# Patch embedding in 98 tiles of 128 patches across image borders, and v's product in the bank of o

## The reference, cut to what matters

```python
patches = patchify(images)                       # 64 x 196 patches x 768
hidden = einsum('npd,hd->nph', patches, W_lin) + b_lin
h = concatenate([cls, hidden], axis=1)           # 64 x 197 tokens x 192
h = h + attention(layernorm(h))                  # 12 heads of 16, q and k normalised by head
h = h + experts(layernorm(h))                    # gate, 8 routed experts and a shared one
```

## Time and profile before

| | |
|---|---|
| median of two runs | 1674.95 us (1672.44 and 1677.46) |
| the profiled execution | 1680.21 us, its span 1678.0 us |
| mean granted clock of TensorE in it | 0.984 |
| PE, DVE, ACT, POOL busy, share of the span | 96%, 76%, 59%, 40% |
| first stage / second stage | about 950 us / about 728 us |

### The profile page before, as it was taken

One profiled execution on the slowest core, in us unless ns is written; L12 is line 12 of the kernel. 1 busy time (PEld: TensorE's weight loads), 2 busy tenths in 40 slices (PEclk: granted clock), 3 DMA queues, 4 the chain that ended last, 5 costly groups with the idle time before them and its releaser, 6 DMA issues. The chain is left out here.

```text
span 1678.0 us, 44146 instructions
## 1 busy us (share of the span) xinstructions
PE 1611.4 (96%) x16714; PEld 1104.3 (66%) x16714; DVE 1275.9 (76%) x3610; ACT 987.5 (59%) x2038; POOL 676.0 (40%) x758
## 2 busy tenths in 40 slices
PE   4999999999999999999998799999999999999998
PEld 4777777777777777777776455555555555555555
DVE  5787777777777777777775488888888878888877
ACT  2777777777777777777766344454545454444543
POOL 2333333333333333333332155554545545555543
PEclk8999999999999999999998599999999999999999
DMA  7233333333333333333310111112121211111110
GB/s 242 69 78 78 78 78 78 78 78 78 78 78 78 78 78 78 78 78 78 106 42 19 30 42 40 56 39 57 36 61 33 58 39 45 52 42 55 34 35 16
DMA packets 97695, 108.11 MB, mean 64 GB/s; under 512 B 61323, under 2 KB 74286, under 8 KB 97358
## 3 DMA queue, kind: packets, MB, share of 16 engines
q1 hardware_dynamic: 88270, 85.83, 17.3%
q0 software_dynamic: 9216, 19.47, 7.6%
HBM read 92.44 MB, written 19.37 MB: 67 GB/s over the span
## 5 line engine op out<-in xcount | busy, mean ns | idle before, releaser
L1407 POOL TENSOR_TENSOR in_lo<-inner,in_hi 128x512 f16<-128x512 f32 (+1 forms) x225 | 259.2, 1152 | 354.5 <-ACT act L1314 342.0
L919 POOL CAST qk_strips<-qk_norm 99x768 f16<-99x768 f32 x128 | 104.9, 820 | 583.6 <-DVE qk_norm L776 583.6
L605 ACT ACTIVATE prob<-ps_sc 99x792 f32<-99x792 f32 x384 | 303.7, 828 | 6.2 <-PE ps_sc L416 2.8
L1322 ACT ACTIVATE in_hi<-inner 128x512 f16<-128x512 f32 (+1 forms) x225 | 140.3, 623 | 198.3 <-DVE inner L1345 198.3
L1363 DVE SCALAR_TENSOR_TENSOR acc<-ps_y,comb,acc 128x192 f32<-128x192 f32 (+1 forms) x700 | 242.0, 408 | 0.3 <-PE ps_y L1286 0.3
L1314 ACT ACTIVATE act<-ps_h 128x512 f32<-128x512 f32 (+1 forms) x225 | 132.0, 587 | 182.0 <-PE ps_h L1270 182.0
L1345 DVE SCALAR_TENSOR_TENSOR inner<-ps_h,act 128x512 f32<-128x512 f32 (+1 forms) x225 | 152.9, 680 | 113.0 <-ACT act L1314 110.6
L1284 PE MATMUL ps_y<-w_hi,in_hi 128*128 128x192 f16 (+1 forms) x900 | 224.2, 249 | 3.1 <-DVE acc L1363 2.8
L1286 PE MATMUL ps_y<-w_hi,in_lo 128*128 128x192 f16 (+1 forms) x900 | 221.4, 246 | 0.0
L1285 PE MATMUL ps_y<-w_lo,in_hi 128*128 128x192 f16 (+1 forms) x900 | 221.4, 246 | 0.0
L354 PE MATMUL ps_hid<-lin_hi,x_hi 128*99 128x192 f16 x768 | 194.1, 253 | 18.8 <-DVE x_lo L724 10.5
(11 more groups left out here) (167 smaller groups left out, 3818.0 us busy)
## 6 DMA issues: line engine op xcount, KB each, us to landing
xin<-xp SPq DMA_DIRECT2D x64, 594.0 KB, 4.3
x_hi<-xp POOLq DMA_DIRECT2D x64, 297.0 KB, 4.0
hidden_dram<-h SPq DMA_DIRECT2D x64, 147.0 KB
hin<-hidden_dram SPq DMA_DIRECT2D x24, 384.0 KB, 3.4
out<-acc SPq DMA_DIRECT2D x24, 384.0 KB, 2.7
w_f<-w SPq DMA_DIRECT2D x1, 2304.0 KB, 9.1
yT_hi<-y_hi SPq DMA_TRANSPOSE x100, 2.4
yT_lo<-y_lo SPq DMA_TRANSPOSE x100, 2.4
```

What stands on the lines that cost most here:

```text
L605: act.activation(prob[quad][:, places].rearrange("p h m s -> p h (m s)"), ps_sc[0:TR, places, 0:2 * SLOTS], ACT.Exp, scale=D ** -0.5 / (SQ ...
L1407: pool.tensor_tensor(in_lo[b][:, 0:N], inner[b][:, 0:N], in_hi[b][:, 0:N], ALU.subtract).then_inc(inlo_done, 1)
```

## The change

The 64 x 196 patches are taken as one list of 12544 and cut into 98 tiles of 128, across the borders of images. Each tile is embedded in two halves of nine products (three chunks each), 1764 products in all in place of 2304, with a 128x128 stationary piece. PE does two halves ahead of the steps and then three per step, four in steps 14, 31 and 46: one in slot a, one in slot b, the rest in slot c, which are the three places where a third of an image was embedded before. `hid` is now 128x192 and holds one tile, so the first half of a tile waits until DVE has taken the tile before it out (`h_done`).

DVE's `hidden` now writes a tile's rows to `h_rows` (four buffers). SP moves them from there by DMA into the rows of `h` of each image (`place`: two or three DMAs per tile), and the layer norm of an image waits for these DMAs (`h_in`). The class token's row of each of the eight `h` buffers is written once, at the start. DVE's `split` is on half tiles, 384 columns, three per step instead of two of 594, and one of them now stands between `residual` and the second `qk_variance`. Loads are per tile: 98 instead of 64, of 384 KB in place of 594 KB (float32).

v's product moves to columns 198 to 389 of `ps_o`, the bank in which `attend` accumulates, and is made in two halves of five products with a copy each; the first waits until ACT has copied the first third of o out of the bank (`oT_out`), the second until DVE has copied the first.

```diff
+TILES = IMAGES * PATCHES // 128
+HALF = PATCHES // 2
+AHEAD = 2
+EXTRA = (14, 31, 46)
...
-        hid = ps_hid[0:TR, 0:2 * C].rearrange("p (t c) -> p t c", t=2)
+        hid = ps_hid[:, 0:C]
+        v_ps = ps_o[0:TR, SLOTS:SLOTS + C]
...
+        def halves_of(step):
+            first = AHEAD + 3 * step + sum(step > e for e in EXTRA)
+            count = 4 if step in EXTRA else 3
+            return [u for u in range(first, first + count) if u < 2 * TILES]
+        def slots_of(step):
+            us = halves_of(step) + [None] * 4
+            return us[0:1], us[1:2], us[2:4]
...
+            def load(j):
+                if j > 3:
+                    sp.wait_ge(xlo_done, 2 * (j - 4) + 2)
+                sp.dma_start(xin[j % 4][:], xp[j]).then_inc(x_in[j % 4], 16)
+            def place(u):
+                if u is None or u % 2 == 0:
+                    return
+                j = u // 2
+                sp.wait_ge(h_done, j + 1)
+                for n, t, row, to, rows_here in pieces_of(j):
+                    if n >= HB:
+                        sp.wait_ge(h2_done, n - HB + 1)
+                    sp.dma_start(h[n % HB][to:to + rows_here, t, :],
+                                 h_rows[j % 4][row:row + rows_here, :]).then_inc(h_in[n % HB], 16)
...
+                a, b, c = slots_of(k.c)
+                if k.c == 0:
+                    place(1)
+                else:
+                    for u in slots_of(k.c - 1)[2]:
+                        place(u)
+                for j in range(loaded(k.c - 1), loaded(k.c)):
+                    load(j)
+                place(a[0])
+                place(b[0])
                 if k.back(5).active():
                     store(k.back(5))
-                if k.back(-3).active():
-                    load(k.back(-3))
...
-            def embed(n, part):
-                hi, lo = x_hi[n.mod(3)], x_lo[n.mod(2)]
-                if part == 0:
-                    pe.wait_ge(xlo_done, n.times(2, 2))
-                    if n.c == 0:
+            def embed(us):
+                for u in us:
+                    if u is None:
+                        continue
+                    j, half_no = u // 2, u % 2
+                    pe.wait_ge(xlo_done, u + 1)
+                    if u == 0:
                         pe.wait_ge(lin_split, 1)
-                    if reached(n.times(1)):
-                        pe.wait_ge(h_done, n.times(1))
-                    if reached(n.times(1, -1)):
-                        pe.wait_ge(v_set, n.times(1, -1))
-                for j in range(4 * part, 4 * part + 4):
-                    t, k = j // PCHUNKS, j % PCHUNKS
-                    s = slice(t * TR, (t + 1) * TR)
-                    pe.matmul(hid[:, t, :], hi[:, k, s], lin_hi[:, k, :], start=(k == 0), stop=False)
-                    pe.matmul(hid[:, t, :], hi[:, k, s], lin_lo[:, k, :], start=False, stop=False)
-                    last = pe.matmul(hid[:, t, :], lo[:, k, s], lin_hi[:, k, :], start=False,
-                                     stop=(k == PCHUNKS - 1))
-                if part == 2:
-                    last.then_inc(hid_done, 1)
+                    if half_no == 0 and j > 0:
+                        pe.wait_ge(h_done, j)
+                    for k in range(3 * half_no, 3 * half_no + 3):
+                        pe.matmul(hid, x_hi[j % 4][:, k, :], lin_hi[:, k, :], start=(k == 0), stop=False)
+                        pe.matmul(hid, x_hi[j % 4][:, k, :], lin_lo[:, k, :], start=False, stop=False)
+                        last = pe.matmul(hid, x_lo[j % 2][:, k, :], lin_hi[:, k, :], start=False,
+                                         stop=(k == PCHUNKS - 1))
+                    last.then_inc(half_done, 1)
...
-            def values(n, embedded):
-                if embedded.active():
-                    pe.wait_ge(h_done, embedded.times(1, 1))
-                for t in range(2):
-                    last = from_xT(hid[:, t, :], t, slice(2 * C, 3 * C))
-                last.then_inc(v_done, 1)
+            def values(n, t, attended):
+                if t == 0 and attended.active():
+                    pe.wait_ge(oT_out, attended.times(QUADS, 1))
+                if reached(n.times(2, t)):
+                    pe.wait_ge(v_set, n.times(2, t))
+                from_xT(v_ps, t, slice(2 * C, 3 * C)).then_inc(v_done, 1)
...
                 if quad == 0:
-                    pe.wait_ge(v_set, n.times(1, 1))
+                    pe.wait_ge(v_set, n.times(2, 2))
+                if quad == 1 and n.back(-1).active():
+                    pe.wait_ge(v_set, n.times(2, 4))
...
-                if n1.active():
-                    embed(n1, 1)
+                a, b, c = slots_of(k.c)
+                embed(a)
...
-                if n1.active():
-                    embed(n1, 2)
+                embed(b)
...
-                    values(n2, n1)
+                    values(n2, 0, n3)
                     if n4.active():
...
                     transpose_qk(n2, 0, 0)
...
-                if k.active():
-                    embed(k, 0)
+                if n2.active():
+                    values(n2, 1, n3)
+                embed(c)
...
-            def split(n, half_no):
-                i = n.times(1)
+            def split(u):
+                if u >= 2 * TILES:
+                    return
+                j, half_no = u // 2, u % 2
                 if half_no == 0:
-                    dve.wait_ge(x_in[n.mod(3)], 16 * (i // 3 + 1))
-                    dve.wait_ge(xhi_in[n.mod(3)], 16 * (i // 3 + 1))
-                    if reached(n.times(1, -1)):
-                        dve.wait_ge(hid_done, n.times(1, -1))
+                    dve.wait_ge(x_in[j % 4], 16 * (j // 4 + 1))
+                    dve.wait_ge(xhi_in[j % 4], 16 * (j // 4 + 1))
+                if u > 3:
+                    dve.wait_ge(half_done, u - 3)
                 ks = slice(3 * half_no, 3 * half_no + 3)
-                dve.tensor_tensor(x_lo[n.mod(2)][:, ks, :], xin[n.mod(3)][:, ks, :], x_hi[n.mod(3)][:, ks, :],
+                dve.tensor_tensor(x_lo[j % 2][:, ks, :], xin[j % 4][:, ks, :], x_hi[j % 4][:, ks, :],
                                   ALU.subtract).then_inc(xlo_done, 1)
-            def hidden(n):
-                q = n.mod(HB)
-                if n.c == 0:
-                    dve.wait_ge(consts_a_loaded, 16 * len(consts_a))
-                    dve.wait_ge(consts_set, 1)
-                dve.wait_ge(hid_done, n.times(1, 1))
-                if reached(n.times(1, 1 - HB)):
-                    dve.wait_ge(h2_done, n.times(1, 1 - HB))
-                dve.scalar_tensor_tensor(out=h[q][:], in0=hid, scalar=1.0 / SW, in1=biascls[:],
-                                         op0=ALU.mult, op1=ALU.add).then_inc(h_done, 1)
+            def hidden(us):
...
+                    j = u // 2
...
+                    dve.wait_ge(half_done, u + 1)
+                    for n, t, row, to, rows_here in (pieces_of(j - 4) if j > 3 else ()):
+                        dve.wait_ge(h_in[n % HB], 16 * arrivals[n])
+                    dve.scalar_tensor_tensor(out=h_rows[j % 4][:], in0=hid, scalar=1.0 / SW, in1=bias[:],
+                                             op0=ALU.mult, op1=ALU.add).then_inc(h_done, 1)
             def hidden_stats(n):
                 q = n.mod(HB)
-                dve.wait_ge(h_done, n.times(1, 1))
+                dve.wait_ge(h_in[q], 16 * arrivals[n.times(1)])
...
-            def v_copy(n):
+            def v_copy(n, t):
                 p = n.mod(2)
-                dve.wait_ge(v_done, n.times(1, 1))
+                dve.wait_ge(v_done, n.times(2, t + 1))
                 if reached(n.times(QUADS, -QUADS)):
                     dve.wait_ge(av_done, n.times(QUADS, -QUADS))
-                own = v[p][:].rearrange("p t h e -> p (t h) e")[:, :, 0:D]
-                dve.tensor_scalar(own, ps_hid[0:TR, 0:2 * C].rearrange("p (h d) -> p h d", d=D), 1.0 / SS, None,
+                dve.tensor_scalar(v[p][:, t, :, 0:D], v_ps.rearrange("p (h d) -> p h d", d=D), 1.0 / SS, None,
                                   ALU.mult).then_inc(v_set, 1)
...
+                a, b, c = slots_of(k.c)
+                ahead = [u + 3 for u in halves_of(k.c)] + [2 * TILES] * 3
                 if n5.active():
                     o_out(n5, 1)
+                hidden(slots_of(k.c - 1)[2] if k.c > 0 else (1,))
                 if 0 <= k.c - FIRST_PIECE - 1 < PIECES:
                     mixture_piece(k.c - FIRST_PIECE - 1)
...
-                    split(k, 1)
+                split(ahead[0])
                 if n3.active():
                     kT_copy(n3, 1)
+                hidden(a)
                 if n2.active():
                     qk_variance(n2, 0)
                 if n2.active():
                     qk_normalise(n2, 0)
-                if n1.active():
-                    hidden(n1)
+                hidden(b)
...
                 if n5.active():
                     residual(n5)
+                split(ahead[1])
```

(71 more changed lines are left out.)

46 lines of the change are left out of this document (23 added, 23 removed).

## The result

The changed kernel took 1782.32 us (1778.86 to 1785.78, two runs) against 1674.95: a ratio of 1.064 with a 95% interval from 1.053 to 1.075. The forecast was 1728, within 1695 to 1770. The sign was right. The rise is +107 instead of +53, and it falls outside the range. Of all executions reported here one was slow, 6467.69 us of the kernel with the copy of o moved; that kernel's median without it is 1753.33.

What follows compares the result with a forecast made beforehand. PE was the bound, 97.73% busy, but within a PE-DVE-ACT-PE ring. Steps gave 32 x 0.32 + 28 x 1.34 = 47.8, fourth halves 2.2, start and end +3: +53 on 1674.95, so 1728 us, range 1695 to 1770.

Steps and rivals of the forecast that it cites:

- rival A: PE alone is the bound and its relief of 44.8 us reaches the end: 1630 us; chance 0.06.
- the ring: Chain PE, DVE, ACT, PE from projection to third scores; DVE's half split counts in full, 0.47 us a step.
- rival B: The half split's shift of 0.47 is swallowed, 60 x 0.47 = 28 us fall away: 1700 us; chance 0.12.
- Odd steps: In 28 steps slot b waits for hidden behind the copy of k: first scores +1.34 us instead of +0.32.
- Row moves: Rows sent by SP's DMAs land before DVE comes to the statistics: counted 0.
- rival C: PE's clock falls to 1.2 GHz in one step of four, 35 us more: 1763 us; chance 0.15.
- rival D: Row DMAs take 2 us more; statistics and residual slip 1.5 us in 32 steps, +48: 1776 us; chance 0.05.
- xnorm's second half at 0.76: On DVE, ahead of the first q/k transposes: making xnorm takes 0.76 us, read from the earlier trace.
- the end of DVE's stretch: DVE's work from v's second half through o's norm, ahead of the first q/k transposes, ends 7.36 us behind the projection.
- The wait for o's bank: v's first half waits for ACT's copy of o; PE ends at 3.98, ahead of third scores at 4.01: no cost.
- The full 90 us: By the bank rule alone, moving v costs PE 1.5 us a step, 60 x 1.5 = 90 us: sum +143.
- The start, +4: At the start, weights' preparation stands behind four tiles' splits and the second tile's embedding: +4 us (ends 0 and 7).

Runs made afterwards that it cites:

- the later kernel: Weights' preparation on DVE ahead of the splits and of hidden of slot a in the first step, against the kernel with the variance first: 1678.55 us.
- three moves: Each alone against the changed kernel: xnorm's second half ahead of v's copy, 1755.49; hidden ahead of k's second copy, 1758.32; half split ahead of v's copy, 1754.04 us.

## Why the prediction was wrong, step by step

*Right.* PE's relief did not reach the end (rival A). The half split stands on the ring in full: 0.47 x 60 = 28 forecast, 28.3 measured by moving it; nothing swallowed it (rival B). Odd steps are longer by 1.07 through `hidden` behind the copy of k (forecast 1.02). Row moves cost nothing in a steady step. The clock did not fall to its lower level (rival C: 0.98 to 1.00 in the windows), and rival D's late rows occurred once, at the start, not in 32 steps.

*The step that failed: xnorm's second half at 0.76.* It was read from the earlier trace rows, where DVE came to xnorm ahead of GpSimd's subtraction. The change puts the smaller xnorm operation just behind the subtraction's start: 1.11, so 0.35 more on the path to the first q/k transposes. With the subtraction short the same stretch takes 0.51: DVE saves 0.60 and a step 0.50, 60 x 0.50 = 30 us (measured -30.7, which brings the time to 1751.64, inside the range). Moving xnorm away from a whole subtraction gives the same steps of 14.30. I followed PE, DVE and ACT, and never asked what GpSimd would be doing beside a moved DVE operation.

The Trainium skill, SBUF — State Buffer, Who interferes with whom, says that DVE in a mode that uses two port pairs contends with GpSimd for the shared pair, that `tensor_scalar`, which makes xnorm, can enter such a mode, and that whoever issues first keeps the pair for its whole instruction while the other is blocked. The trace agrees with the blocking: 0.91 beside a subtraction of 0.92, 0.31 beside one of 0.25. In which mode xnorm ran, no run here shows.

*A sum.* The terms written for the end of DVE's stretch add up to 7.44, not 7.36. The 7.36 holds only if the copy of v keeps DVE for 0.27 and not for the 0.35 stated; it kept DVE for 0.28 (514.71 to 514.99), so the total was right and the term was not.

*The wait for o's bank, taken at nothing.* v's transposes ended just behind 4.01, not just ahead of it: 0.09 a step, some 5 us. The full 90 us that the prediction set beside this did not come.

*In steps, in sum.* The means are 15.34 measured and 14.78 forecast: 0.56 x 60 = 33.6. The nine steps with the large pieces of the mixture's weights exceed others of their kind by 0.95 instead of before's 0.32: 5.7. Together 39.3, of the 38.5 by which the middle stretch missed; single late steps (18.30 the longest, in which a half split waited 1.85) and shorter last steps, some 7 us each, nearly cancel. Why the weight steps grew was not tried.

*The start, +4 against +14.2.* The first image's statistics began at 27.28 instead of 22.98, so 4.3 as forecast, but mostly by luck: moved forward by 4.8 in the later kernel, the preparation of the weights brought these statistics only 1.2 earlier (28.31 instead of 29.52) and the first residual 0.05. 7.0 of the miss are the rows behind the weights' load: I looked for row moves only in steady steps. The remaining 3 us and the 4 at the end were not separated.

*The range* held x tiles and row moves at nothing, and had no case for work on GpSimd.

## What to carry to other kernels

When an operation is moved on one engine, look at what every engine that shares a resource with it does at its new place; a duration read at the old place holds only for the old neighbours. Mend waits one at a time and look again: each of three moves was worth 24 to 28 us, and behind them stood further waits, for a load in GpSimd's queue and then for a copy of v. Work taken off the busiest engine pays only when all of these have gone: 0.75 us a step became +1.4, then -0.57.

## What the hardware showed that was not expected

The two engines held each other up before the change as well, and the 0.76 of the forecast had part of it inside. DVE's timeline in the kernel before, for both halves of one image:

```profile
520.15 0.37 DVE L757 TENSOR_SCALAR xnorm<-h,meanvar,h_rstd 99x192 f32<-99x192 f32 x1
...
522.61 0.62 DVE L757 TENSOR_SCALAR xnorm<-h,meanvar,h_rstd 99x192 f32<-99x192 f32 x1
523.15 0.30 DVE L759 TENSOR_SCALAR xnorm<-h,meanvar,h_rstd 99x64 f32<-99x64 f32 x1
```

And GpSimd's:

```profile
517.77 0.91 POOL L921 TENSOR_TENSOR qk_strips<-qk_norm,qk_strips 99x384 f16<-99x384 f32 x1
...
522.29 0.82 POOL L919 CAST qk_strips<-qk_norm 99x768 f16<-99x768 f32 x1 [3.61 <-DVE qk_norm L776]
523.19 1.72 POOL L921 TENSOR_TENSOR qk_strips<-qk_norm,qk_strips 99x384 f16<-99x384 f32 x1
```

The larger xnorm operation starts inside GpSimd's cast and takes 0.62; at 520.15, with GpSimd idle, it took 0.37. GpSimd's subtraction starts inside the smaller one, has the split of 0.77 beside it next, and takes 1.72 instead of 0.91; which of the two held it was not tried. No engine's idle time is put down to it there. So before, GpSimd lost 0.8 us of slack and DVE 0.25; after, DVE loses 0.60, on the path.
